# Two threshold digits per attention tile, and an expert layer written out

## The chip, the cores and the metric

The kernel runs on one core of a Trainium2 chip. The metric is the device time of one execution in microseconds. Before the change it was 1450.71 us, the median of three runs (1446.56 to 1451.18).

## The reference, cut to what matters

Input x has shape (4, 1024, 256). Four layers follow one another, each added to x: a cross attention, an expert layer with the two best experts of each token, a second cross attention with 16 heads over 77 keys, and an expert layer in which each expert chooses its tokens. The change touches the last two.

```python
def _L1_ffn_ref(x, gate_w, w_gate, w_up, w_down):
    k = S // E * CAPACITY                      # 256 tokens for each of 8 experts
    affinity = softmax(einsum('bsd,ed->bse', x, gate_w)).transpose(0, 2, 1)
    gating, idx = jax.lax.top_k(affinity, k)
    x_in = x[bidx, idx]
    h = silu(einsum('bekd,eid->beki', x_in, w_gate)) * einsum('bekd,eid->beki', x_in, w_up)
    x_e = einsum('beki,edi->bekd', h, w_down)
    return zeros_like(x).at[bidx, idx].add(gating[..., None] * x_e)
```

So before the first expert can start, the 256th largest affinity of every pair of batch and expert must be known.

## The kernel before, in words

**The search.** The four batches are handled as two halves (q = 0 and 1) of two batches each, so a search finds 16 thresholds (2 batches, 8 experts) at once. The threshold is built as the bits of a float, ten digits of three bits. For a digit, `count` on VectorE compares 1024 affinities a partition with a candidate and adds up (L1515, L1516); `choose_pe` on TensorE adds the passed candidates with a matmul of one column (L1439); `choose_dve` on VectorE turns the sum into the digit and the next candidate (L1523 to L1526). Each step waits for the one before it. After digit 9 come four more exchanges between the two engines: THR (threshold to all partitions, two masks, L1441, L1532), RANKS (prefix sums of the masks, L1445 to L1449, slot numbers and the one-hot arrays hotA and hotC, L1536 to L1544), FILL (matmul of the one-hots, L1455, own tokens, L1546 to L1549) and TURN (L1459, the index table gidx, L1554). GpSimd then gathers the rows of an expert with gidx (L2030).

**The attention.** `in_order` writes out 32 tiles of 128 rows with no loop. Each engine runs a list of named steps (PE_ORDER, DVE_ORDER and so on, L1580 to L1588), each with a lag: in iteration j the step works on tile j minus lag. TensorE runs about two iterations ahead of VectorE. The first search runs in it: its softmax at tile 19, `count` of digit 0 at tile 26, digits 0 to 4 with tiles 27 to 31 (FIRST_DIGIT, lag 2 on VectorE, with the scores on TensorE). Digits 5 to 9, THR and RANKS are in the table TAIL, after the last scores (`tail_a` and `tail_b`), while the last tiles are finished; I call this stretch the drain. FILL and TURN come in `topk_tensor` and `topk_vector`, after the last tile. There the second search (q = 1) also starts with its softmax and first count.

In an iteration VectorE computes, in this order: statistics and normalising, the residual of tile t (L1848, reads psO1), low halves of probabilities (L1817), maxima of the scores (L1825, L1834), the digit, the count. TensorE: transposes out, turn2, tail_a, outputs0, transposes in, scores0 (with the digit's matmul ahead), outputs1, turn0, outputs2, turn1, scores1, tail_b, logits. The logits (psL1) share a PSUM bank with psO1, and wait for the residual that reads it.

**The expert layer.** Sixteen items (expert and batch half), a step j does: `up` of item j-2 (8 blocks f0 to f7, 12 matmuls each), `transposes` of item j-1, `down` of item j-3 (4 blocks n0 to n3). ScalarE and VectorE split the weights in high and low f16 parts (L2112, L2172, L2122, L2181) and compute the hidden rows (L2136, L2196, L2209). `pipeline` writes steps 0 to 5 out, runs steps 6 to 13 in a loop of two turns of four steps, and writes out the rest. The second search is placed by the table LATER: (step, block) to exchange. Its exchange on TensorE comes right after that block; on VectorE after the block's hidden rows (f), ahead of the eight low parts of the down weights (n1) or behind them (n2, n3).

Of the kernel before, what the change touches and what calls it, by code (L numbers as in the profile page):

```python
# [31 lines left out]
P = 128  # L32
# [113 lines left out]
def program(nc, a, out, tab, n0_rows, x1_rows, n_rows):  # L146
    ctx = ExitStack()
    with ctx:
# [1266 lines left out]
        D_MASK = D_THR + 2  # L1415
        D_HOT = D_MASK + 7
        D_LIST = D_HOT + 3
# [92 lines left out]
        def count(dve, ch, q, i):  # L1510
# [5 lines left out]
            ch(dve.tensor_scalar(passed[:], cnt1[:], CAP - 0.5, None, ALU.is_ge))  # L1516

        def choose_dve(dve, ch, q, p, bank0, bank1):

# [14 lines left out]
            elif p == RANKS:  # L1534
# [4 lines left out]
                ch(dve.tensor_scalar(sc_[:], sloti[:], 15, None, ALU.bitwise_and))  # L1539
                nums = iota16[:].unsqueeze(1).to_broadcast([P, NI * RB, 16])  # L1540
                ch(dve.tensor_tensor(hotA[:], sa[:].unsqueeze(2).to_broadcast([P, NI * RB, 16]), nums, ALU.is_equal))
                ch(dve.tensor_tensor(hotC[:], sc_[:].unsqueeze(2).to_broadcast([P, NI * RB, 16]), nums, ALU.is_equal))
                values = hotC[:].rearrange("p (i c) n -> p i (c n)", i=NI)
                ch(dve.tensor_tensor(values, values, tokv[:].unsqueeze(2).to_broadcast([P, NI, RB * 16]), ALU.mult))  # L1544
            elif p == FILL:
# [5 lines left out]
            else:  # L1551
                for b in range(2):
# [11 lines left out]
        ROWS_AT = ((0, 23), (1, 24), (0, 24), (1, 25))  # L1564
        TAIL = {(27, "a"): 5, (27, "b"): 6, (28, "a"): 7, (28, "b"): 8, (29, "a"): 9, (29, "b"): THR, (30, "a"): RANKS}
        c_one = sem("c_one")
# [4 lines left out]
        PE_ORDER = [("transposes_out", 5), ("turn2", 3), ("tail_a", 6), ("outputs0", 3), ("transposes_in", 0), ("scores0", 1),  # L1571
                    ("outputs1", 3), ("turn0", 2), ("outputs2", 3), ("turn1", 2), ("scores1", 0), ("tail_b", 6), ("logits", 6)]
        ACT_ORDER = [("exps1", 2), ("probs_high0", 3), ("shares_exp", 5), ("exps0", 2), ("probs_high1", 3), ("copy_out", 5),
                     ("high_in", 0), ("weights_high", 0), ("shares_copy", 5), ("probs_high2", 3)]
        DVE_ORDER = [("stats_in", 0), ("normalise_out", 6), ("moments_in", 0), ("residual", 5), ("shares_max", 5), ("probs_low0", 4),
                     ("tail_a", 7), ("stats_out", 5), ("moments_out", 5), ("largest1", 2), ("reciprocals", 3), ("probs_low1", 4),
                     ("maxima1", 2), ("low_in", 1), ("probs_low2", 4), ("largest0", 2), ("digit", 2), ("maxima0", 2),
# [124 lines left out]
        def attn1_tensor(pe):  # L1702
# [14 lines left out]
            def scores(half):  # L1717
                def run(t, par):
                    pe.wait_ge(c_xl, t + 1)
                    wait(pe, c_exp[half], t)  # L1720
                    if (half, t) in ROWS_AT:
                        rows_pe(pe, 0, ROWS_AT.index((half, t)), inA[2 * half:2 * half + 2])
                    if half == 0 and t >= FIRST_DIGIT:
                        choose_pe(pe, 0, t - FIRST_DIGIT, inA[0], inA[1])
                    for q in (2 * half, 2 * half + 1):
                        for k in range(KD):
                            at = bass.ds((t // (S // P)) * (KD * CK) + (k * CK + q * QK), QK)
                            last = mm3(pe, psS1[:, q, 0:QK], xh1[:, par, k, :], xl1[:, par, k, :],
                                       M1hf[:, at], M1lf[:, at], k == 0, k == KD - 1)
                    last.then_inc(c_sc[half], 1)  # L1730
                return run

            def logits(t, par):
                pe.wait_ge(c_xe, t + 1)
                wait(pe, c_res, before(t, "logits", "outputs0", PE_ORDER, T))
                for k in range(KD):
                    last = pe.matmul(psL1[:, bass.ds(t * E, E)], xt1[:, par, k, :], gts1[:, k, :], start=(k == 0), stop=(k == KD - 1))
                last.then_inc(c_lg, 1)
# [24 lines left out]
            def tail(name):  # L1763
                def run(t, par):
                    if (t, name) not in TAIL:
                        return
                    for n in range(2):
                        pe.wait_ge(c_exp[n], T)
                    choose_pe(pe, 0, TAIL[t, name], drain0, drain1)
                return run  # L1770
            M1hf = M1h[:].rearrange("p b k c -> p (b k c)")
            M1lf = M1l[:].rearrange("p b k c -> p (b k c)")
            N1f = N1[:].rearrange("p b c d -> p (b c d)")
            steps = dict(tail_a=tail("a"), tail_b=tail("b"), transposes_in=transposes(0), transposes_out=transposes(1), scores0=scores(0), scores1=scores(1),
                         turn0=turn(0), turn1=turn(1), turn2=turn(2), logits=logits,
# [6 lines left out]
        def attn1_vector(dve):  # L1782
# [59 lines left out]
            def residual(t, par):  # L1842
                row = X[:, bass.ds(t, 1), :].rearrange("p t d -> p (t d)")
                dve.wait_ge(c_av[2], t + 1)
                if t == 19:
                    dve.wait_ge(c_lg, T // 2)
                    soft_max(dve, ch, 0)
                dve.scalar_tensor_tensor(row, psO1, thx1[:, 0:1], row, ALU.mult, ALU.add).then_inc(c_res, 1)  # L1848

# [11 lines left out]
            def digit(t, par):  # L1861
                if t >= FIRST_DIGIT:
                    choose_dve(dve, ch, 0, t - FIRST_DIGIT, inA[0], inA[1])

            def counts(t, par):
                if t >= FIRST_DIGIT - 1:
                    count(dve, ch, 0, t - FIRST_DIGIT + 1)

            def tail(name):
                def run(t, par):  # L1870
                    if (t, name) not in TAIL:
                        return
                    p = TAIL[t, name]
                    choose_dve(dve, ch, 0, p, drain0, drain1)
                    if p + 1 < DIGITS:
                        count(dve, ch, 0, p + 1)
                return run
# [22 lines left out]
            def weights_low(t, par):  # L1900
                f = t - 4
                if not 0 <= f < FT1:
# [6 lines left out]
            ch = Chain(dve, k_dve, 0, KSTEPS)  # L1909
            steps = dict(shares_max=shares_max, shares_div=shares_div, digit=digit, count=counts, tables=tables,  # L1910
                         tail_a=tail("a"), tail_b=tail("b"), weights_low=weights_low,
                         probs_low0=probs_low(0), probs_low1=probs_low(1), probs_low2=probs_low(2),
# [4 lines left out]
            in_order(dve, steps, DVE_ORDER, T, straight=True)  # L1917
            return ch

# [43 lines left out]
        second0, second1 = psXb[:, 0, :], psXb[:, 1, :]  # L1963
        LATER = {(2, "f2"): 0, (2, "f5"): 1, (3, "f2"): 2, (3, "f5"): 3, (3, "n1"): 4, (3, "n2"): 5, (3, "n3"): 6,
                 (4, "f2"): 7, (4, "f5"): 8, (4, "n1"): 9, (4, "n2"): THR, (4, "n3"): RANKS, (5, "f5"): FILL, (5, "n1"): TURN}

# [17 lines left out]
        def topk_tensor(pe):  # L1984
            choose_pe(pe, 0, FILL, drain0, drain1)
            choose_pe(pe, 0, TURN, drain0, drain1)
            for n in range(ROWS):
                rows_pe(pe, 1, n, [psYb[:, n, k * P:(k + 1) * P] for k in range(2)])

        def topk_vector(dve, first):  # L1990

            second = Chain(dve, k_dve, 1, KSTEPS)
            dve.wait_ge(c_lg, T)
            choose_dve(dve, first, 0, FILL, drain0, drain1)
            choose_dve(dve, first, 0, TURN, drain0, drain1)
            soft_max(dve, second, 1)
# [54 lines left out]
        def ffn1_tensor(pe):  # L2051
            def transposes(j, ph):
                par = ph % 2
                pe.wait_ge(d_in[par], 16 * NT * (j // 2) + 16 * NT)
                wait(pe, d_xl, KD * j)
                p = later(j + 1, "f5") if isinstance(j, int) else None
                if p is not None:
# [40 lines left out]
            for n in range(2):  # L2098
                pe.wait_ge(c_exp[n], T)
            pipeline(pe, NB1, DD, [(2, up), (1, transposes), (3, down)], unroll=4)  # L2100

        def ffn1_scalar(act):
# [58 lines left out]
            work += [(1, up_high(f, False)) for f in range(FT1)] + [(2, down_high(f)) for f in range(FT1)]  # L2161
            pipeline(act, NB1, DD, work + [(3, results)], unroll=4)

        def ffn1_vector(dve, ch):
# [47 lines left out]
            def choose(lag, name):  # L2212
                def run(j, ph):
# [4 lines left out]
                    if p + 1 < DIGITS:  # L2218
                        count(dve, ch, 1, p + 1)
                return run  # L2220
            work = [(2, hidden(0)), (1, up_low(0, True))]
            for f in range(1, FT1):
                work += [(2, hidden(f)), (2, hidden_low(f - 1)), (1, up_low(f, True)), (2, choose(2, f"f{f - 1}"))]
            work += [(2, hidden_low(FT1 - 1)), (1, rows_low)]
            work += [(1, up_low(f, False)) for f in range(FT1)]
            work += [(3, choose(3, "n1"))] + [(2, down_low(f)) for f in range(FT1)] + [(3, choose(3, "n2")), (3, choose(3, "n3"))]
            pipeline(dve, NB1, DD, work, unroll=4)

        with nc.Block() as block:
# [36 lines left out]
            def _(dve):  # L2266
                attn0_vector(dve)
                ffn0_vector(dve)
                prep_vector(dve)
                first = attn1_vector(dve)  # L2270
                second = topk_vector(dve, first)
                ffn1_vector(dve, second)
# [51 lines left out]
```

## Time and profile before

| | us |
|---|---|
| median of three runs | 1450.71 |
| the profiled execution's own time | 1452.21 |
| its span, first to last instruction | 1450.5 |
| TensorE busy in the span | 1317.3 (91%) |
| VectorE busy | 912.1 (63%) |
| ScalarE busy | 759.9 (52%) |
| GpSimd busy | 625.2 (43%) |

The profile is of one execution. The granted clock of TensorE is 1.00 at full speed and 0.50 at half. By the trace the second attention's tiles run up to about 834 us, the drain to 893.6, the expert layer from there to the end. A busy share says how much an engine works, not whether anyone waits for it; for that the waits and the order in time are read.

### The profile page before, as it was taken

How to read it: one execution, taken by the hardware profiler on the slowest of the kernel's cores; microseconds unless marked ns; L12 is line 12 of the kernel's file. 1: busy time of each engine (PE TensorE's matmuls, PEld its weight loads, DVE VectorE, ACT ScalarE, POOL GpSimd, SP SyncE). 2: the span in 40 equal slices, each digit the busy share in tenths (PEclk: the TensorE clock that was granted, in tenths of full speed). 3: DMA queues.
4: the chain of work that ended last, by engine and by line, in shares of the span. 5: the costliest groups of instructions: out<-in, count | busy, mean ns of one | idle time of the engine just before them, and what ended most of it. 6: DMA issues, size and time to landing. Idle time of an engine off the chain costs nothing.

```text
span 1450.5 us, 29512 instructions
## 1 busy us (share of the span) xinstructions
PE 1317.3 (91%) x9858; PEld 988.9 (68%) x9859; DVE 912.1 (63%) x2123; ACT 759.9 (52%) x2313; POOL 625.2 (43%) x664
## 2 busy tenths in 40 slices
PE   6877699999999987999999965898999989999997
PEld 3766588889999856888888853355656646665555
DVE  2887664565554585778777855777655646655551
ACT  3765322433323365988878812444555646655552
POOL 2187777656666531554444413123233332233313
PEclk8665699999999989999999976999999999999998
DMA  5658445653333341000200102233333333444422
GB/s 145 215 146 201 76 50 70 134 87 62 61 65 61 52 124 59 23 31 31 95 31 30 33 29 76 102 117 117 117 117 117 117 118 117 123 159 158 130 44 30
DMA packets 81547, 133.20 MB, mean 92 GB/s; under 512 B 24662, under 2 KB 71260, under 8 KB 76316
## 3 DMA queue, kind: packets, MB, share of 16 engines
q1 hardware_dynamic: 51132, 93.92, 19.8%
q0 software_dynamic: 29312, 37.57, 15.6%
q8 instruction: 64, 1.05, 0.3%
q14 instruction: 47, 0.39, 0.1%
q10 hardware_dynamic: 992, 0.27, 0.1%
HBM read 95.08 MB, written 36.65 MB: 91 GB/s over the span
## 4 chain that ended last, share of the span: by engine, by line
PE 71%; DVE 10%; DMA 7%; issue 4%; POOL 4%; ACT 3%; SPq 1%; POOLq 0%; ACTq 0%; DVEq 0%
PE psG L124 5%; PE psG L125 5%; PE psG L126 5%; PE psU L124 5%; PE psU L126 5%; PE psU L125 5%; PE psYb L126 3%; PE psYb L124 3%; PE psYb L125 3%; DMA stage<-in_w 2%; PE psS L124 2%; PE psS L125 2%; PE psS L126 2%; PE psP L1747 2%; PE psOL L124 2%
## 5 line engine op out<-in xcount | busy, mean ns | idle before, releaser
L2045 POOL DMA_INDIRECT out_x<-yo,gidx x64 | 107.6, 1681 | 343.3 <-ACT yo L2147 327.3
L2196 DVE SCALAR_TENSOR_TENSOR hid<-psU,sil 128x512 f32<-128x512 f32 x128 | 88.4, 691 | 198.1 <-ACT sil L2136 197.8
L2136 ACT ACTIVATE sil<-psG 128x512 f32<-128x512 f32 x128 | 76.4, 597 | 217.5 <-PE psU L126 217.5
L980 POOL DMA_INDIRECT x_rows<-yo,tabs x78 | 124.4, 1594 | 94.9 <-ACT yo L1052 71.1
L1673 ACT ACTIVATE pr<-psS,mx 128x77 f32<-128x77 f32 x512 | 158.8, 359 | 0.8 <-DVE mx L1834 0.8
L125 PE MATMUL psYb<-W1dl,hh 128*128 128x256 f16 x512 | 140.4, 274 | 0.0
L124 PE MATMUL psYb<-W1dh,hh 128*128 128x256 f16 x512 | 140.4, 274 | 0.0
L126 PE MATMUL psYb<-W1dh,hl 128*128 128x256 f16 x512 | 140.3, 274 | 0.0
L1079 DVE SCALAR_TENSOR_TENSOR hid<-psU,sil 128x512 f32<-128x512 f32 x78 | 53.8, 690 | 127.7 <-ACT sil L1043 127.6
L1673 ACT ACTIVATION_READ_ACCUMULATOR pr<-psS,mx 128x1 f32 x512 | 123.7, 242 | 0.0
L1043 ACT ACTIVATE sil<-psG 128x512 f32<-128x512 f32 x78 | 46.5, 596 | 133.1 <-PE psU L126 133.1
L970 POOL DMA_INDIRECT bx<-n_rows,tabs x78 | 82.5, 1058 | 26.0 <-issue 21.9
L124 PE MATMUL psOL<-N,pt 128*128 128x256 f16 x320 | 89.2, 279 | 3.1 <-DVE pt L1817 3.1
L124 PE MATMUL psG<-bxh,Wh 128*128 128x256 f16 x312 | 85.6, 274 | 4.6 <-DVE bxl L1070 4.6
L2030 POOL DMA_INDIRECT gx<-n_rows,gidx x64 | 64.0, 1001 | 59.5 <-DVE gxl L2189 24.5
L125 PE MATMUL psOL<-N,pt 128*128 128x256 f16 x320 | 89.3, 279 | 0.0
L126 PE MATMUL psOL<-N,pt 128*128 128x256 f16 x320 | 89.2, 279 | 0.0
L2209 DVE TENSOR_TENSOR hl<-hid,hh 128x512 f16<-128x512 f32 x128 | 87.7, 685 | 1.7 <-ACT hh L2155 0.2
L124 PE MATMUL psU<-bxh,Wh 128*128 128x256 f16 x312 | 85.6, 274 | 0.0
L125 PE MATMUL psG<-bxl,Wh 128*128 128x256 f16 x312 | 85.6, 274 | 0.0
L126 PE MATMUL psU<-bxh,Wl 128*128 128x256 f16 x312 | 85.6, 274 | 0.0
L125 PE MATMUL psU<-bxl,Wh 128*128 128x256 f16 x312 | 85.6, 274 | 0.0
(403 smaller groups left out, 4189.5 us busy)
## 6 DMA issues: line engine op xcount, KB each, us to landing
w1u<-in_w SPq DMA_DIRECT2D x16, 2048.0 KB, 7.5
w1d<-in_w SPq DMA_DIRECT2D x16, 1024.0 KB, 8.1
stage<-in_w SPq DMA_DIRECT2D x8, 1536.0 KB, 8.7
X<-in_x SPq DMA_DIRECT2D x8, 512.0 KB, 8.9
n_rows<-xc SPq DMA_DIRECT2D x8, 512.0 KB, 9.5
x_rows<-X SPq DMA_DIRECT2D x8, 512.0 KB, 12.0
X<-x_rows SPq DMA_DIRECT2D x8, 512.0 KB, 8.1
out_x<-X SPq DMA_DIRECT2D x32, 128.0 KB, 1.7
```

What stands on the lines that cost most here:

```text
L124: pe.matmul(o, lh, rh, start=first, stop=False)
L125: pe.matmul(o, lh, rl, start=False, stop=False)
L126: return pe.matmul(o, ll, rh, start=False, stop=stop)
L970: pool.indirect_dma_start(bx[:, par, n, :], None, n0_rows[:, :], bass.IndirectOffsetOnAxis(tabs[:, j, n, 0:1], 0)).then_inc(b_in[par], 16)
L980: pool.indirect_dma_start(x1_rows[:, :], bass.IndirectOffsetOnAxis(tabs[:, j, n, 0:1], 0), yo[:, par, n, :], None, compute_op=ALU.add).the ...
L1079: dve.scalar_tensor_tensor(hid[:, half, :, :], psU[half][:, :, :], SH / (SX * SW), sil[:, half, :, :], ALU.mult, ALU.mult).then_inc(b_hid[ ...
L1673: ins = act.activation(pr1[:, par, h * LK:(h + 1) * LK], psS1[:, q, i * LK:(i + 1) * LK], ACT.Exp, bias=mx1[:, h:h + 1], scale=1.0 / (SX * ...
L2030: pool.indirect_dma_start(gx[:, j % 2, n, :], None, n_rows[0:2 * S * (j // E + 1), :], bass.IndirectOffsetOnAxis(gidx[:, half, col:col + 1 ...
L2045: pool.indirect_dma_start(out_rows[:, :], bass.IndirectOffsetOnAxis(gidx[:, half, col:col + 1], 0), yo1[:, j % 2, n, :], None, compute_op= ...
L2136: act.activation(sil1[:, f % 2, :], psG1[f % 2][:], ACT.Silu, scale=1.0 / (SX * SW)).then_inc(d_sil, 1)
L2196: dve.scalar_tensor_tensor(hid1[:, f % 2, :], psU1[f % 2][:], SH / (SX * SW), sil1[:, f % 2, :], ALU.mult, ALU.mult).then_inc(d_hid, 1)
L2209: dve.tensor_tensor(hl1[:, par, f, :], hid1[:, f % 2, :], hh1[:, par, f, :], ALU.subtract).then_inc(d_hl, 1)
```

## The change: what it does

First, in the attention's last five tiles a search takes an even digit where it took its only one before, and an odd digit in a new step `digit_odd`: on TensorE after turn1 and ahead of scores1, on VectorE after the residual, followed by `count_odd` after the first low half. Digits 0, 2, 4, 6, 8 come at tiles 27 to 31, digits 1, 3, 5, 7, 9 with the iterations of the residuals of tiles 25 to 29. The odd sum is written to psL1's bank, so the residual waits for the digit's matmul and the logits wait until the digit is read. THR, RANKS, FILL and TURN move into the drain. The one-hot work of RANKS (three operations on 2048 elements) becomes six on 1024, `one_hot_half`.

Second, the expert layer is written out on TensorE, ScalarE and VectorE (straight=True).

Third, the second search moves from steps 2 to 5 to steps 3 to 7, three exchanges a step, and its six one-hot halves go one behind each of the blocks f0 to f5 of step 7.

```diff
-        D_HOT = D_MASK + 7
+        D_HOT = D_MASK + 10
+        def one_hot_half(dve, ch, n):
+            half = slice((n % 2) * (NI * RB // 2), (n % 2 + 1) * (NI * RB // 2))
+            nums = iota16[:].unsqueeze(1).to_broadcast([P, NI * RB // 2, 16])
+            if n < 2:
+                ch(dve.tensor_tensor(hotA[:, half], sa[:, half].unsqueeze(2).to_broadcast([P, NI * RB // 2, 16]), nums, ALU.is_equal))
+            elif n < 4:
+                ch(dve.tensor_tensor(hotC[:, half], sc_[:, half].unsqueeze(2).to_broadcast([P, NI * RB // 2, 16]), nums, ALU.is_equal))
+            else:
+                values = hotC[:, half].rearrange("p (i c) n -> p i (c n)", i=NI // 2)
+                tiles = slice((n % 2) * (NI // 2), (n % 2 + 1) * (NI // 2))
+                ch(dve.tensor_tensor(values, values, tokv[:, tiles].unsqueeze(2).to_broadcast([P, NI // 2, RB * 16]), ALU.mult))
...
-        TAIL = {(27, "a"): 5, (27, "b"): 6, (28, "a"): 7, (28, "b"): 8, (29, "a"): 9, (29, "b"): THR, (30, "a"): RANKS}
+        FIRST_ODD = 25
+        TAIL_PE = {(27, "a"): THR, (28, "a"): RANKS, (29, "b"): FILL, (30, "b"): TURN}
+        TAIL_DVE = {(27, "a"): THR, (28, "b"): RANKS, (29, "b"): FILL, (30, "b"): TURN}
+        def even_of(t):
+            return 2 * (t - FIRST_DIGIT) if 0 <= t - FIRST_DIGIT < DIGITS // 2 else None
+        def odd_of(t):
+            return 2 * (t - FIRST_ODD) + 1 if 0 <= t - FIRST_ODD < DIGITS // 2 else None
...
-                    ("outputs1", 3), ("turn0", 2), ("outputs2", 3), ("turn1", 2), ("scores1", 0), ("tail_b", 6), ("logits", 6)]
+                    ("outputs1", 3), ("turn0", 2), ("outputs2", 3), ("turn1", 2), ("digit_odd", 3), ("scores1", 0), ("tail_b", 6), ("logits", 6)]
...
-        DVE_ORDER = [("stats_in", 0), ("normalise_out", 6), ("moments_in", 0), ("residual", 5), ("shares_max", 5), ("probs_low0", 4),
-                     ("tail_a", 7), ("stats_out", 5), ("moments_out", 5), ("largest1", 2), ("reciprocals", 3), ("probs_low1", 4),
+        DVE_ORDER = [("stats_in", 0), ("normalise_out", 6), ("moments_in", 0), ("residual", 5), ("digit_odd", 5), ("shares_max", 5), ("probs_low0", 4),
+                     ("count_odd", 5), ("tail_a", 7), ("stats_out", 5), ("moments_out", 5), ("largest1", 2), ("reciprocals", 3), ("probs_low1", 4),
...
+                if odd_of(t + 3) is not None:
+                    pe.wait_ge(k_dve, read_at(0, odd_of(t + 3)))
...
+                if odd_of(t) is not None:
+                    dve.wait_ge(k_pe, ROWS + odd_of(t) + 1)
                 dve.scalar_tensor_tensor(row, psO1, thx1[:, 0:1], row, ALU.mult, ALU.add).then_inc(c_res, 1)
...
+                    if p == RANKS:
+                        for n in range(6):
+                            one_hot_half(dve, ch, n)
...
-        LATER = {(2, "f2"): 0, (2, "f5"): 1, (3, "f2"): 2, (3, "f5"): 3, (3, "n1"): 4, (3, "n2"): 5, (3, "n3"): 6,
-                 (4, "f2"): 7, (4, "f5"): 8, (4, "n1"): 9, (4, "n2"): THR, (4, "n3"): RANKS, (5, "f5"): FILL, (5, "n1"): TURN}
+        LATER = {(3, "f4"): 0, (3, "n1"): 1, (3, "n2"): 2, (4, "f4"): 3, (4, "n1"): 4, (4, "n2"): 5,
+                 (5, "f4"): 6, (5, "n1"): 7, (5, "n2"): 8, (6, "f4"): 9, (6, "n1"): THR, (6, "n2"): RANKS,
+                 (7, "n1"): FILL, (7, "n2"): TURN}
+        ONE_HOT_STEP = 7
...
         def topk_tensor(pe):
-            choose_pe(pe, 0, FILL, drain0, drain1)
-            choose_pe(pe, 0, TURN, drain0, drain1)
...
-            choose_dve(dve, first, 0, FILL, drain0, drain1)
-            choose_dve(dve, first, 0, TURN, drain0, drain1)
...
-            pipeline(pe, NB1, DD, [(2, up), (1, transposes), (3, down)], unroll=4)
+            pipeline(pe, NB1, DD, [(2, up), (1, transposes), (3, down)], unroll=4, straight=True)
...
+            def one_hot(f):
+                def run(j, ph):
+                    if j + 2 == ONE_HOT_STEP and f < 6:
+                        one_hot_half(dve, ch, f)
+                return run
...
-                work += [(2, hidden(f)), (2, hidden_low(f - 1)), (1, up_low(f, True)), (2, choose(2, f"f{f - 1}"))]
+                work += [(2, hidden(f)), (2, hidden_low(f - 1)), (1, up_low(f, True)), (2, choose(2, f"f{f - 1}")), (2, one_hot(f - 1))]
```

## Rows read from the trace of the kernel before

**Rows 1.** The page's part 4, the chain's shares by engine.

```profile
PE 71%; DVE 10%; DMA 7%; issue 4%; POOL 4%; ACT 3%; SPq 1%; POOLq 0%; ACTq 0%; DVEq 0%
```

**Rows 2.** Windows, one attention tile: length, busy by engine, clock, DMA share, GB/s.

```profile
817.54:825.98 8.44, 8.44 (x76) 7.21 (x74) 7.22 (x21) 6.91 (x38) 3.33 (x5) 1.00 0.09 31
```

**Rows 3.** Timeline of VectorE: start, length, operation, and idle time with its releaser.

```profile
824.17 0.42 DVE L1810 SCALAR_TENSOR_TENSOR xl<-psXar,xh 128x256 f16<-128x256 f32 x1 [0.66 <-ACT xh L1648]
...
825.26 0.81 DVE L1825 TENSOR_REDUCE psS<-psS 128x8 f32<-128x616 f32 x1 [0.34 <-PE psS L126]
...
833.41 0.81 DVE L1825 TENSOR_REDUCE psS<-psS 128x8 f32<-128x616 f32 x1 [1.45 <-PE psS L126]
834.13 0.15 DVE L1523 TENSOR_SCALAR dig<-psS 128x1 int32<-128x1 f32 x1
...
836.35 0.41 DVE L1804 TENSOR_SCALAR xn<-X,mv,rs 128x256 f32<-128x256 f32 x1
```

**Rows 4.** Timeline of TensorE in the drain and at the first expert matmul.

```profile
842.03 0.36 PE L124 MATMUL psOL<-N,pt 128*128 128x256 f16 x1 [2.20 <-DVE pt L1817]
...
877.85 1.89 PE L1455 MATMUL psS<-hotC,hotA 128*128 128x128 f16 x16 [6.73 <-DVE hotC L1544]
...
893.61 0.61 PE L124 MATMUL psG<-gxh,upAh 128*128 128x512 f16 x1 [2.08 <-DVE gxl L2189]
```

**Rows 5.** Timeline of the drain, GpSimd and VectorE.

```profile
842.20 1.91 POOL L1620 TENSOR_TENSOR pn<-pr,sum 128x1024 f32<-128x1024 f32 x1
...
869.54 0.42 DVE L1536 SCALAR_TENSOR_TENSOR slot<-psS,mask 128x256 f32<-128x256 f32 x1 [2.60 <-PE psS L1449]
...
870.85 2.29 DVE L1541 TENSOR_TENSOR hotA<-sa,iota 128x2048 f16<-128x2048 int32 x1
...
882.80 1.12 POOL L2030 DMA_INDIRECT gx<-n_rows,gidx  x1 [16.37 <-DVE gidx L1554]
```

**Rows 6.** Timeline of TensorE: the transposes in expert steps 3 to 6.

```profile
945.54 1.04 PE L2061 MATMUL psXb<-ident,gx 128*128 128x128 f32 x8
...
983.12 1.04 PE L2061 MATMUL psXb<-ident,gx 128*128 128x128 f32 x8
...
1026.33 1.06 PE L2061 MATMUL psXb<-ident,gx 128*128 128x128 f32 x8
...
1058.47 1.04 PE L2061 MATMUL psXb<-ident,gx 128*128 128x128 f32 x8
```

**Rows 7.** Timeline of TensorE: its waits in expert steps 3 to 5.

```profile
922.18 0.61 PE L124 MATMUL psG<-gxh,upBh 128*128 128x512 f16 x1 [4.53 <-DVE gxl L2189]
...
957.40 0.16 PE L1439 MATMUL psXb<-passed,same 128*128 128x1 bf16 x1 [2.94 <-DVE passed L1516]
...
993.48 0.20 PE L1441 MATMUL psXb<-ident,thrb 16*128 16x16 f32 x1 [1.43 <-DVE thrb L1528]
...
1007.08 0.61 PE L124 MATMUL psG<-gxh,upBh 128*128 128x512 f16 x1 [3.98 <-DVE hid L2196]
```

**Rows 8.** Timeline of SyncE's load issues (one a step), and TensorE at step 10.

```profile
1163.64 0.33 SPq L1583 DMA_DIRECT2D w1u<-in_w  x1
...
1171.20 0.61 PE L124 MATMUL psG<-gxh,upAh 128*128 128x512 f16 x1 [4.99 <-issue]
...
1203.53 0.33 SPq L1583 DMA_DIRECT2D w1u<-in_w  x1
...
1331.82 0.33 SPq L1583 DMA_DIRECT2D w1u<-in_w  x1
...
1363.90 0.33 SPq L1583 DMA_DIRECT2D w1u<-in_w  x1
```

**Rows 9.** Timeline of VectorE in expert steps 3 and 6.

```profile
949.12 1.28 DVE L2189 SCALAR_TENSOR_TENSOR gxl<-psXb,gxh 128x512 f16<-128x512 f32 x2
...
955.14 0.15 DVE L1523 TENSOR_SCALAR dig<-psXb 128x1 int32<-128x1 f32 x1
...
1061.30 1.28 DVE L2189 SCALAR_TENSOR_TENSOR gxl<-psXb,gxh 128x512 f16<-128x512 f32 x2
```

More of the change, by code:

```diff
@@ L1539, in choose_dve @@
                 ch(dve.tensor_scalar(sc_[:], sloti[:], 15, None, ALU.bitwise_and))
[L1540 to L1544, printed above, removed]
             elif p == FILL:
@@ L1723, in run @@
                     if half == 0 and t >= FIRST_DIGIT:
-                        choose_pe(pe, 0, t - FIRST_DIGIT, inA[0], inA[1])
+                        choose_pe(pe, 0, even_of(t), inA[0], inA[1])
                     for q in (2 * half, 2 * half + 1):
@@ L1764, in run @@
                 def run(t, par):
-                    if (t, name) not in TAIL:
+                    if (t, name) not in TAIL_PE:
                         return
@@ L1768, in run, with digit_odd @@
                         pe.wait_ge(c_exp[n], T)
-                    choose_pe(pe, 0, TAIL[t, name], drain0, drain1)
+                    choose_pe(pe, 0, TAIL_PE[t, name], drain0, drain1)
                 return run
+            def digit_odd(t, par):
+                if odd_of(t) is not None:
+                    choose_pe(pe, 0, odd_of(t), psL1, None)
             M1hf = M1h[:].rearrange("p b k c -> p (b k c)")
@@ L1773, in attn1_tensor @@
             N1f = N1[:].rearrange("p b c d -> p (b c d)")
-            steps = dict(tail_a=tail("a"), tail_b=tail("b"), transposes_in=transposes(0), transposes_out=transposes(1), scores0=scores(0), scores1=scores(1),
+            steps = dict(tail_a=tail("a"), tail_b=tail("b"), digit_odd=digit_odd, transposes_in=transposes(0), transposes_out=transposes(1), scores0=scores(0), scores1=scores(1),
                          turn0=turn(0), turn1=turn(1), turn2=turn(2), logits=logits,
@@ L1847, in residual @@
                     soft_max(dve, ch, 0)
+                if odd_of(t) is not None:
+                    dve.wait_ge(k_pe, ROWS + odd_of(t) + 1)
                 dve.scalar_tensor_tensor(row, psO1, thx1[:, 0:1], row, ALU.mult, ALU.add).then_inc(c_res, 1)
@@ L1861, in digit, with digit_odd, count_odd @@
             def digit(t, par):
-                if t >= FIRST_DIGIT:
-                    choose_dve(dve, ch, 0, t - FIRST_DIGIT, inA[0], inA[1])
+                if even_of(t) is not None:
+                    choose_dve(dve, ch, 0, even_of(t), inA[0], inA[1])
             def counts(t, par):
-                if t >= FIRST_DIGIT - 1:
-                    count(dve, ch, 0, t - FIRST_DIGIT + 1)
+                if t == FIRST_DIGIT - 1:
+                    count(dve, ch, 0, 0)
+                if even_of(t) is not None:
+                    count(dve, ch, 0, even_of(t) + 1)
+            def digit_odd(t, par):
+                if odd_of(t) is not None:
+                    choose_dve(dve, ch, 0, odd_of(t), psL1, None)
+            def count_odd(t, par):
+                if odd_of(t) is not None and odd_of(t) + 1 < DIGITS:
+                    count(dve, ch, 0, odd_of(t) + 1)
             def tail(name):
                 def run(t, par):
-                    if (t, name) not in TAIL:
+                    if (t, name) not in TAIL_DVE:
                         return
-                    p = TAIL[t, name]
+                    p = TAIL_DVE[t, name]
                     choose_dve(dve, ch, 0, p, drain0, drain1)
-                    if p + 1 < DIGITS:
-                        count(dve, ch, 0, p + 1)
+                    if p == RANKS:
+                        for n in range(6):
+                            one_hot_half(dve, ch, n)
                 return run
@@ L1910, in attn1_vector @@
             steps = dict(shares_max=shares_max, shares_div=shares_div, digit=digit, count=counts, tables=tables,
+                         digit_odd=digit_odd, count_odd=count_odd,
                          tail_a=tail("a"), tail_b=tail("b"), weights_low=weights_low,
@@ L1917, in attn1_vector @@
             in_order(dve, steps, DVE_ORDER, T, straight=True)
-            return ch
         l1.close()
@@ L1984, in topk_tensor, with topk_vector @@
         def topk_tensor(pe):
-            choose_pe(pe, 0, FILL, drain0, drain1)
-            choose_pe(pe, 0, TURN, drain0, drain1)
             for n in range(ROWS):
                 rows_pe(pe, 1, n, [psYb[:, n, k * P:(k + 1) * P] for k in range(2)])
-        def topk_vector(dve, first):
+        def topk_vector(dve):
             second = Chain(dve, k_dve, 1, KSTEPS)
             dve.wait_ge(c_lg, T)
-            choose_dve(dve, first, 0, FILL, drain0, drain1)
-            choose_dve(dve, first, 0, TURN, drain0, drain1)
             soft_max(dve, second, 1)
@@ L2055, in transposes @@
                 wait(pe, d_xl, KD * j)
-                p = later(j + 1, "f5") if isinstance(j, int) else None
+                p = later(j + 1, "f4") if isinstance(j, int) else None
                 if p is not None:
@@ L2161, in ffn1_scalar @@
             work += [(1, up_high(f, False)) for f in range(FT1)] + [(2, down_high(f)) for f in range(FT1)]
-            pipeline(act, NB1, DD, work + [(3, results)], unroll=4)
+            pipeline(act, NB1, DD, work + [(3, results)], unroll=4, straight=True)
         def ffn1_vector(dve, ch):
@@ L2226, in ffn1_vector @@
             work += [(3, choose(3, "n1"))] + [(2, down_low(f)) for f in range(FT1)] + [(3, choose(3, "n2")), (3, choose(3, "n3"))]
-            pipeline(dve, NB1, DD, work, unroll=4)
+            pipeline(dve, NB1, DD, work, unroll=4, straight=True)
         with nc.Block() as block:
@@ L2269, in _ @@
                 prep_vector(dve)
-                first = attn1_vector(dve)
-                second = topk_vector(dve, first)
+                attn1_vector(dve)
+                second = topk_vector(dve)
                 ffn1_vector(dve, second)
```

## The prediction

> **What bounds the kernel now.** I read the chain of waits, then windows tile by tile, then the timelines of the drain and of expert steps 2 to 10. The chain's split by engine [rows 1] says TensorE 71%, VectorE only 10%, so a change to VectorE's work pays only where VectorE's searches are what TensorE waits for. There are four kinds of places.
>
> In an attention tile TensorE has no idle time: 8.44 of 8.44 us, VectorE 7.22, in the tile from 817.54 [rows 2]. VectorE's true waits there are 0.66 and 0.34 us, and 1.45 us in the last tile, where it waits for the scores [rows 3]. In the drain after the last tile (834.1 to 893.6) the order turns round: TensorE waits for digits and residuals that stand behind counts, then 6.73 us for the one-hot arrays, and the experts' first matmul starts at 893.61 [rows 4]. In the expert layer a step costs 32.08 us once it runs freely (1331.82 to 1363.90, written-out code) [rows 8]; the step from 945.54 to 983.12 takes 37.58 and the next 43.21 [rows 6], and step 10 takes 39.89 (1163.64 to 1203.53), with 4.99 us in which TensorE waits for nothing that the profile shows [rows 8].
>
> **Part 1: two digits a tile.** One digit is read, applied and counted in 2.15 us of VectorE (834.13 to 836.35, less 0.08 for the maxima between) [rows 3]. Before, digits 0 to 3 are read a tile apart each, digit 4 at 834.13 in the last tile, and digits 5 to 9 come after it. After, digits 0, 2, 4, 6, 8 are read at those points and 1, 3, 5, 7 between them: four more of 2.15, 8.6 us. VectorE's waits in the four tiles are 1.00, 1.00, 1.00 and 1.45 [rows 3], 4.45 in all, and they cover that much. So digit 8 is read at 834.13 + 8.6 - 4.45 = 838.25: the tiles grow by 4.1 us, from about 8.6 to 9.7.
>
> The new waits. TensorE takes the odd digit after its transposes and before the next scores, and must wait for VectorE's count; behind it stand the scores (1.57), logits, transposes and outputs of 1.3, some 4.5 us up to the next even digit. VectorE needs 4.2 us from that count to the next (normalising, residual, odd digit, one low half, count), then 2.8 us more before it wants the scores, which are there at 6.1. So each side keeps about 0.9 us of slack, and the period is VectorE's sum. The residual's new wait on TensorE costs nothing: 1.1 us of normalising lies between. TensorE idles 1.0 to 1.4 us a tile. Bounds: +2 (TensorE's gaps in the records give cover too) to +8.6 (no cover).
>
> **Part 2: the drain.** Clock at 0 when digit 8 is read. Count of digit 9 to 2.2; residual, digit 9 and its broadcast to 3.6; one low half to 4.2; threshold transposed and two masks to 5.4; statistics to 6.0. GpSimd's root and the normalising (1.91 and 0.69, first of them in [rows 5]) to 9.6. Transposes and outputs (1.9) to 11.5, residual, logits, transposes to 13.3, ranks 1.7 to 15.0. Before, each step of this kind had a digit round of 2.15 in it. VectorE then takes slots (869.54 to 870.85, 1.3) and six halves. A whole one-hot pass is 2.29 for 2048 elements and a 256-element one 0.42 [rows 5]; 1024 by the line between them is 1.22, and with 0.03 between instructions the six take 7.5: to 24.0. The halves stand ahead of the last residual, so outputs of tile 31 are hidden under them, and the logits, the transpose of tile 30 and the fill come after: residual 24.8, logits and transpose 26.2, fill 28.2 (1.89 at half clock [rows 4]), own tokens 30.1, normalise, transpose and turn 31.3, indices 32.0, gather 32.3. Before, the gather starts at 882.80 [rows 5], 48.7 after its digit 4. So 16.4 less, and 12.3 less net of the tiles: gather at 870.5.
>
> From gather to first expert matmul it was 10.8 us (882.80 to 893.61). The second search's softmax now starts 0.5 us later against it (it waits for the last logits), and has 1.9 us of slack. The down-weight load, before at 871.20, far ahead of the gather, now goes out beside it. It took 4.9 us alone, so at most the gather's first half meets it: I take 0.3, bounds 0 and 2. First matmul near 881.6; gain 12.0, bounds 7 and 16.
>
> The row gives half of 2.29, 1.15, if nothing is paid per instruction. Against this change speaks the Trainium skill (VectorE: DVE Perf Modes, "The TRN2 errata — SBUF-src ops pay a fixed extra latency per instruction"): about 151 cycles at 0.96 GHz come with every instruction, so many small tiles pay many times. By that, an estimate, a half is 1.224 us and six cost 7.3 before gaps against 6.9 by halving: 0.5 us lost by the split. It changes the total by less than its uncertainty.
>
> **Part 3: expert layer written out.** The loop covers steps 6 to 13 in two turns of four, so TensorE jumps back once, at step 10: 4.99 us of nothing, then half clock (first matmul 0.61 instead of 0.38) [rows 8]. Against the free step this is 39.89 - 32.08 = 7.8 us. No VectorE, ScalarE or load is late there. Written out it goes. The free 32.08 is of a step without a loop, so straight code has no price of its own that shows; ends 0 and 7.8, I take 7.8.
>
> **Part 4: second search in steps 3 to 7.** Step 2 loses its two digits (4.3 us of VectorE beside early weight conversions). TensorE waited 4.53 before 922.18 [rows 7]; without the digits VectorE's last hidden row starts 1.35 earlier and the 0.19 stall at 911 goes: 1.5 saved, the rest of the wait is the transposes' own path.
>
> Steps 3, 4, 5 each have a digit at f4, n1, n2. That at f4 is hidden: VectorE waits 1.3 a block there and recovers in two. The pair n1, n2 isn't: VectorE reads n1 only after eight low conversions (955.14), so n2 at TensorE waited 2.94 (957.40) [rows 7]. Now no digit at f5 delays this. Free, the low rows start 2.83 after the transposes (1061.30 against 1058.47), with f5 3.58 (949.12 against 945.54) [rows 6, 9]: 0.75 earlier, so the wait is 2.2. Does the clock fall? After 2.20 idle at 842.03 matmuls went from 0.27 to 0.36, then 0.42 [rows 4]; after 1.43 at 993.48 it held [rows 7]. I say it falls, 1.75 more each as in the 3.5 us at half clock after 957.4. Three steps: 3 x 3.95 = 11.9. Step 6: threshold 0.7 (masks instead of a count), ranks 1.3; step 7: fill 1.1, wait 0.6, turn 0.2; its halves of 1.25 fit under the 1.3 of wait a block. Sum 15.8, against (37.58 - 32.08) + (43.21 - 32.08) = 16.6 now, in which the one-hots alone held TensorE 3.98 (1007.08) [rows 7]. Saved 0.8; bounds +6 (clock holds) and -4 (every one falls, halves not quite hidden).
>
> **Sum.** 12.0 + 7.8 + 1.5 + 0.8 = 22.1. The profiled execution took 1452.21 (span 1450.5), 1.5 over the median of 1450.71; applied to the median: 1428.6, I say 1429.
>
> **Rivals.**
> (a) The clock falls in the tiles. TensorE now idles over 1 us in each of four or five tiles; if that is enough to halve its clock, its 8.4 us of work become some 15, and a tile 15.3 instead of 9.7. Four and a half tiles cost 25 and outweigh 22: 1454. It decides at the point where an idle time of 1.0 to 1.4 a tile lowers the granted clock from 1.00. Against: 1.43 at 993.48 didn't. For: such gaps would repeat every tile. 6%.
> (b) The clock holds after 2.2 us waits in steps 3 to 5, and in the drain too: 5.2 and 3 more, 1420 to 1423. 13%.
> (c) The halves, the fill behind the last residual and the load beside the gather eat half of the drain's gain (no VectorE cover in the tiles 4.4, gather 2): 1435 to 1440. 13%.
> (d) The 7.8 isn't the jump. Step 10 is also the first with an expert of the second batch half; then it stays, and 1437. Against: its rows were ready (VectorE had done everything of the step by 1166.3). 7%.
> (e) The change doesn't shorten the drain at all because something older binds (the second search's start, the weight load): gain of 10 only, 1441 or more, up to no change. 6%.
>
> **Chances.** Main case (1424 to 1434) 55%, rivals as above. What can be told from no change is 0.3%, 4.4 us. Below 1446: 0.90; within: 0.04; above 1455: 0.06, mostly (a). Range 1419 to 1441: it takes in (b), (c), (d).
>
> **What would show it.** Digit 8 read near 838.3; TensorE clock 1.00 through the tiles; gather near 870.5 and first expert matmul near 881.6; six 1.2 us passes between 854 and 862, TensorE idle under them; step 10 at 32.1; steps 3 to 5 at about 36, 6 and 7 at 34. Wrong if the tiles take over 10 us each, if TensorE's clock is at half in them, or if step 10 keeps a 5 us gap.

## The result, and the profile after

The changed kernel takes 1424.47 us (median of four, 1421.16 to 1426.59) against 1450.91 before (four runs, 1446.56 to 1451.18). The ratio is 0.9821, 95% interval 0.9803 to 0.9839: 26.4 us faster. Forecast was 1429.

The profiled execution took 1426.59 us with a span of 1424.8. By stage it stands against before like this (each number is a difference of two starts; the first count of the search is the common start, 791.73 before and 794.06 after):

| stretch | before | after | change | forecast |
|---|---|---|---|---|
| start to first count | 791.73 | 794.06 | +2.3 | 0 |
| first count to the last tile's digit | 42.40 | 46.38 | +4.0 | +4.1 |
| that digit to the first gather | 48.67 | 30.98 | -17.7 | -16.4 |
| gather to first expert matmul | 10.81 | 11.30 | +0.5 | +0.3 |
| first expert matmul to step 3's load | 61.64 | 58.07 | -3.6 | -1.5 |
| intervals 4 to 8 | 176.32 | 172.92 | -3.4 | -0.8 |
| interval 10 | 39.89 | 32.07 | -7.8 | -7.8 |

An interval is the time from one up-weight load to the next and has the number of the load that ends it; the loads go out late in a step, so interval 4 holds the down blocks of step 3. A load waits until VectorE has made the low parts of the weights before, so it goes out later where VectorE is late, though TensorE isn't. That is so at step 3's load of before (the parts end at 955.21, it goes out at 955.25): VectorE begins these parts 4.78 us after the transposes before (945.54 [rows 6]) and 4.02 after the change, and 0.8 of the 3.6 us is this. By the transposes, from which the prediction adds, the two lines are -2.8 and -4.2. Before:

```profile
950.32 4.89 DVE L2172 SCALAR_TENSOR_TENSOR upAl<-w1u,upAh 128x512 f16<-128x512 f32 x8
...
1122.62 1.04 PE L2061 MATMUL psXb<-ident,gx 128*128 128x128 f32 x8
```

After:

```profile
931.85 1.04 PE L2096 MATMUL psXb<-ident,gx 128*128 128x128 f32 x8
...
935.87 4.89 DVE L2207 SCALAR_TENSOR_TENSOR upAl<-w1u,upAh 128x512 f16<-128x512 f32 x8
...
1104.77 1.04 PE L2096 MATMUL psXb<-ident,gx 128*128 128x128 f32 x8
```

The first line of the table isn't the change's: the kernels do the same there, and its place moves between profiles of both attentions (789.74 to 794.24 over nine profiles).

The windows of three of the tiles with two digits, from the read of one even digit to the next (columns as in [rows 2]):

```profile
811.99:821.96 9.97, 9.04 (x76) 7.08 (x74) 9.59 (x30) 7.12 (x39) 4.12 (x8) 1.00 0.19 36
821.96:831.52 9.56, 8.90 (x76) 7.12 (x74) 9.18 (x27) 7.02 (x39) 3.32 (x6) 1.00 0.08 27
831.52:840.44 8.92, 8.31 (x71) 6.71 (x70) 8.54 (x26) 6.32 (x36) 3.01 (x6) 1.00 0.10 32
```

The roles of [rows 2] have changed: VectorE (third) is busy 9.59 of 9.97 us with no wait shown, TensorE (first) has 0.9 us idle, and its clock stays at 1.00, the upper of its two levels (2.4 GHz).

The drain on VectorE. To be seen: the last even digit (840.44, answering to 834.13 in [rows 3]), the residual of tile 30 after a wait for its outputs, slots and six halves in a row (two in each line), the residual of tile 31 behind them, the indices.

```profile
840.44 0.15 DVE L1536 TENSOR_SCALAR dig<-psS 128x1 int32<-128x1 f32 x1
...
852.18 0.48 DVE L1874 SCALAR_TENSOR_TENSOR X<-psOL,thx,X 128x256 f32<-128x256 f32 x1 [1.95 <-PE psOL L126]
...
854.88 0.42 DVE L1549 SCALAR_TENSOR_TENSOR slot<-psS,mask 128x256 f32<-128x256 f32 x1
...
856.19 2.48 DVE L1523 TENSOR_TENSOR hotA<-sa,iota 128x1024 f16<-128x1024 int32 x2
858.71 2.48 DVE L1525 TENSOR_TENSOR hotC<-sc_,iota 128x1024 f16<-128x1024 int32 x2
861.22 2.48 DVE L1529 TENSOR_TENSOR hotC<-hotC,tokv 128x1024 f16<-128x1024 f16 x2
863.75 0.41 DVE L1828 TENSOR_SCALAR xn<-X,mv,rs 128x256 f32<-128x256 f32 x1
864.08 0.48 DVE L1874 SCALAR_TENSOR_TENSOR X<-psOL,thx,X 128x256 f32<-128x256 f32 x1
...
870.73 0.41 DVE L1562 TENSOR_SCALAR gidx<-psS 128x16 int32<-128x16 f32 x2 [0.82 <-PE psS L1459]
```

And on TensorE over the same stretch, with waits up to the first expert matmul (not all of them are shown), which answers to 893.61 in [rows 4]:

```profile
853.72 0.27 PE L1445 MATMUL psS<-mask,tri 128*128 128x256 bf16 x1
...
864.70 0.99 PE L1757 MATMUL psOL<-gts,xt 128*128 128x8 f32 x4 [6.58 <-DVE X L1874]
866.00 1.91 PE L1455 MATMUL psS<-hotC,hotA 128*128 128x128 f16 x16
...
878.70 1.94 PE L2096 MATMUL psXb<-ident,gx 128*128 128x128 f32 x8 [0.81 <-DMA gx<-n_rows,gidx]
882.72 0.61 PE L124 MATMUL psG<-gxh,upAh 128*128 128x512 f16 x1 [2.08 <-DVE gxl L2224]
```

TensorE still waits 6.58 us for the one-hot work; the profile gives the residual as the cause, since it stands behind the halves on VectorE. The halves take 856.19 to 863.75, 7.56 us, where three whole passes took 6.95 (870.85 [rows 5] to 877.80): the split costs 0.6. By the Trainium skill (VectorE: DVE Perf Modes, "The TRN2 errata — SBUF-src ops pay a fixed extra latency per instruction") three more instructions were estimated to cost 0.5, and the trace agrees: a fixed cost is there, and 0.6 in all.

The gather starts at 871.42 (882.80 before [rows 5]), where the timeline of GpSimd shows

```profile
871.42 1.12 POOL L2065 DMA_INDIRECT gx<-n_rows,gidx  x1 [5.23 <-DVE gidx L1562]
```

and 7.28 us later TensorE has its rows (878.70), against 6.78 before: the weight load at 872.48 beside it costs at most 0.5.

In the experts, TensorE's waits in steps 3 to 5, which answer to [rows 7]:

```profile
909.41 0.61 PE L124 MATMUL psG<-gxh,upBh 128*128 128x512 f16 x1 [3.54 <-DVE gxl L2224]
...
942.94 0.16 PE L1439 MATMUL psXb<-passed,same 128*128 128x1 bf16 x1 [2.17 <-DVE passed L1516]
...
979.09 0.16 PE L1439 MATMUL psXb<-passed,same 128*128 128x1 bf16 x1 [2.18 <-DVE passed L1516]
...
1013.57 0.16 PE L1439 MATMUL psXb<-passed,same 128*128 128x1 bf16 x1 [2.17 <-DVE passed L1516]
```

Each wait for the count is there, 2.2 us as worked out. What differs is the clock behind them. Windows of TensorE behind the three waits for the count (length, busy, clock, DMA share, GB/s):

```profile
943.00:946.00 3.00, 3.00 (x19) 0.59 0.99 421
...
979.00:982.00 3.00, 2.91 (x27) 1.00 1.01 426
...
1013.50:1016.00 2.50, 2.43 (x24) 1.00 0.99 419
```

After the first wait of 2.17 the clock fell, to 0.59 on average; after those of 2.18 and 2.17 it stayed. So interval 4 takes 36.15 us, intervals 5 and 6 34.5.

### The profile page after: what moved, and what is told of

Same layout as the page of the kernel before. It is cut to its first block, busy times and chain, and to the rows that moved or that the text cites. A ratio compares the mean times of both kernels' runs of the same rounds, so it can differ in the third digit from the quotient of the medians.

```text
span 1424.8 us, 29209 instructions
## 1 busy us (share of the span) xinstructions
PE 1300.5 (91%) x9858; PEld 977.7 (69%) x9859; DVE 914.8 (64%) x2129; ACT 760.5 (53%) x2313; POOL 623.0 (44%) x664
## 3 DMA queue, kind: packets, MB, share of 16 engines
q0 software_dynamic: 29312, 37.57, 15.8%
## 4 chain that ended last, share of the span: by engine, by line
PE 72%; DVE 11%; DMA 5%; POOL 4%; issue 4%; ACT 3%; SPq 0%; POOLq 0%; ACTq 0%; DVEq 0%
PE psG L124 6%; PE psG L126 6%; PE psG L125 6%; PE psU L124 6%; PE psU L125 6%; PE psU L126 6%; PE psYb L124 3%; PE psYb L126 3%; PE psYb L125 3%; PE psS L124 2%; PE psP L1767 2%; DMA stage<-in_w 2%; PE psS L125 2%; PE psS L126 2%; PE psOL L126 2%
## 5 line engine op out<-in xcount | busy, mean ns | idle before, releaser
L124 PE MATMUL psOL<-N,pt 128*128 128x256 f16 x320 | 87.3, 273 | 0.7 <-DVE pt L1841 0.7
L125 PE MATMUL psOL<-N,pt 128*128 128x256 f16 x320 | 87.3, 273 | 0.0
L126 PE MATMUL psOL<-N,pt 128*128 128x256 f16 x320 | 87.2, 273 | 0.0
L126 PE MATMUL psG<-bxh,Wl 128*128 128x256 f16 x312 | 85.7, 275 | 0.0
```

What stands on the lines that cost most here:

```text
L124: pe.matmul(o, lh, rh, start=first, stop=False)
L125: pe.matmul(o, lh, rl, start=False, stop=False)
L126: return pe.matmul(o, ll, rh, start=False, stop=stop)
```

## The experiments

Seven kernels. Steps are timed by the same load intervals, in these texts too where a step's time is given; "first matmul" is the expert layer's first. The time of the kernel before was taken again beside each group of runs: 1450.43 us for e1 to e4, 1448.57 for e5 to e7.

**e1_pe_straight** and **e2_pe_loop2** change the kernel before in one line, TensorE's expert loop:

```diff
-            pipeline(pe, NB1, DD, [(2, up), (1, transposes), (3, down)], unroll=4)
+            pipeline(pe, NB1, DD, [(2, up), (1, transposes), (3, down)], unroll=4, straight=True)   # e1
+            pipeline(pe, NB1, DD, [(2, up), (1, transposes), (3, down)], unroll=2)                  # e2
```

> The kernel before with the expert layer written out on TensorE alone; ScalarE and VectorE keep their loops. Theory (TensorE's own jump back costs the 4.99 us and the half clock after it): step 10 falls from 39.89 to 32.1 us, the whole 7.8 us faster, ratio about 0.9946. Rival 1 (the jump of ScalarE or VectorE holds step 10, or all three do): step 10 stays above 35 us, under 4 us faster. Rival 2 (step 10 is slow as the first with an expert of the second batch half): it stays at 39.9, no change.

Measured: 1443.41 us, ratio 0.9941 (0.9907 to 0.9975). Interval 10 takes 32.07, and the others from 4 on are within 0.2 of before. SyncE's load issues at step 10:

```profile
1163.47 0.33 SPq L1583 DMA_DIRECT2D w1u<-in_w  x1
...
1195.54 0.33 SPq L1583 DMA_DIRECT2D w1u<-in_w  x1
```

So TensorE's loop alone held step 10 ([rows 8]: 39.89). The loops that ScalarE and VectorE kept show no cost there, and the expert of the second batch half isn't it either.

> The kernel before with TensorE's expert loop two steps long instead of four: five turns over steps 6 to 15, four jumps back (at steps 8, 10, 12, 14) instead of one. Theory (each jump back costs TensorE the same): gaps of about 5 us with half clock behind them at steps 8, 10, 12 and 14, 3 x 7.8 = 23 us slower, 1474, ratio 1.016. Rival (the price is that the loop's body of four steps has to be loaded again, and a body half as long needs it less or not): the gaps are clearly under 5 us or absent, and the kernel is between 8 us faster and 5 us slower.

Measured: 1441.91 us, ratio 0.9942 (0.9926 to 0.9957), so my theory falls and the rival holds: with four jumps back in place of one there is no gap at all. Steps 4 to 8 are those of before, and all from 9 to 15 take 32.07 or 32.08.

```profile
1165.84 0.33 SPq L1583 DMA_DIRECT2D w1u<-in_w  x1
...
1197.91 0.33 SPq L1583 DMA_DIRECT2D w1u<-in_w  x1
```

It isn't the jump that costs 5 us, but the jump back over a long body. Part 3 of the profile's page says as much. The instruction packets of queue q8 before, with the short loop, and written out (e1):

```profile
q8 instruction: 64, 1.05, 0.3%
```

```profile
q8 instruction: 48, 0.79, 0.2%
```

```profile
q8 instruction: 61, 1.00, 0.3%
```

Written-out code holds eight steps more than the short loop and reads 13 packets more, some 1.6 a step. The long loop holds four steps fewer than written-out code, which at 1.6 a step would be about 54 packets, but it read 64: its body was loaded again, the short one wasn't. Reading code alone shows no cost, since e1 reads 61 packets and has no gap; the gap comes where TensorE jumps back to code that has to be loaded again. By windows a step has 202 matmuls and about as many weight loads, so four steps are over 1600 instructions and two over 800 (waits and register instructions not counted).

The Trainium skill (Runtime: NRT & Kernel Launch, "Instruction fetch mechanics") has a taken branch stall where its target isn't in the current window of two pages. That only the longer jump stalls agrees with it. Its size of a page, 256 instructions, doesn't: the short body's 800 are more than two such pages, and it didn't stall. The measurement decides; where between the two lengths the limit lies no run here shows.

**e3_attention_only** is the changed attention with the expert layer of before (loops, LATER of before, one-hots in six halves at one place).

> The changed attention with its drain, and the expert layer of before (loops, second search in steps 2 to 5; the one-hot work there in six halves in one place instead of three whole operations). Theory by the trace after: the first expert matmul comes 13.2 us earlier than before, less 0.4 for the halves in step 4: 12.8 us faster, 1438, ratio 0.991. Rival (the time before the changed stage is longer in the changed kernel as such, 2.3 us in the two profiles): 10.5 us faster, and the first count of the search again 2 us later than in the kernel before.

Measured: 1437.97 us, ratio 0.9911 (0.9882 to 0.9940): 12.5 us faster. First count at 790.85, first matmul at 879.56, 88.71 later; before it was 101.88, in the changed kernel 88.66. The 13.2 us belong to the attention part, and the 2.3 us ahead of it to the execution. Its loop over four steps is kept, and interval 10 takes 39.52 us with 64 packets on q8, as before.

**e4_old_later** is the changed kernel with only the second search put back (the diff is cut; its six one-hot halves stand in one place behind RANKS):

```diff
-        LATER = {(3, "f4"): 0, (3, "n1"): 1, (3, "n2"): 2, (4, "f4"): 3, ...
+        LATER = {(2, "f2"): 0, (2, "f5"): 1, (3, "f2"): 2, (3, "f5"): 3, ...   # as before
```

> The changed kernel with the second search back at steps 2 to 5 (its one-hot work in six halves in one place), all else as changed, expert layer written out. Theory by the two traces: the placement is worth 3.6 us in steps 2 and 3 and 3.5 us in steps 4 to 8, so this is 7 us slower than the changed kernel: 1431.5, ratio to before 0.9866. Rival (my prediction's 1.5 + 0.8): 2.3 us slower than the changed kernel, 1427.

Measured: 1428.97 us, ratio 0.9855 (0.9822 to 0.9888), 4.5 by the medians; by the traces 6.7 (first matmul to the end 548.8 against 542.1). The interval is too wide to part 7 from 2.3 by the times; the traces do it. The stretch from the first matmul to the first load and intervals 3 to 8 are 28.0, 33.85, 37.6, 42.1, 32.0, 32.1, 32.1 against 24.9, 33.2, 36.2, 34.5, 34.5, 33.9, 33.9. But 1.4 of the 3.2 us in the first number isn't the placement's: TensorE's clock was at 0.50 for 5.7 us from the first matmul in e4 and for 2.8 in the changed kernel, ahead of the first exchange of the search in either. Without it 5.3 us are left for the placement, near the 4.9 of the two ratios (0.0034 of 1451).

**e5_third_at_f1** takes away what makes TensorE wait at n2:

```diff
-        LATER = {(3, "f4"): 0, (3, "n1"): 1, (3, "n2"): 2, (4, "f4"): 3, (4, "n1"): 4, (4, "n2"): 5,
-                 (5, "f4"): 6, (5, "n1"): 7, (5, "n2"): 8, (6, "f4"): 9, (6, "n1"): THR, (6, "n2"): RANKS,
+        LATER = {(3, "f1"): 0, (3, "f4"): 1, (3, "n1"): 2, (4, "f1"): 3, (4, "f4"): 4, (4, "n1"): 5,
+                 (5, "f1"): 6, (5, "f4"): 7, (5, "n1"): 8, (6, "f1"): 9, (6, "f4"): THR, (6, "n1"): RANKS,
                  (7, "n1"): FILL, (7, "n2"): TURN}
```

> The changed kernel with the second search's third exchange of a step moved from n2 to f1: f1, f4, n1 in steps 3 to 6, fill and turn stay at n1 and n2 of step 7. Theory (TensorE waits at n2 only because n1 is read after eight low conversions, and at f1 a digit hides under 1.3 us of wait a block): the three waits of 2.17 us go, with the 1.7 to 1.8 us of half clock behind one of them, and step 6 loses its wait too: steps 3 to 5 at 32.1 to 32.4 us, step 6 at 33.2, 9 us faster than the changed kernel: 1415.5, ratio to before 0.9758. Rival (VectorE has no room at f1, since it comes late out of the down weights): TensorE waits 1 to 2 us for hidden rows in up, and the gain is under 4 us.

Measured: 1413.17 us, ratio 0.9749 (0.9732 to 0.9766) where the changed kernel has 0.9821: some 10.4 us faster. The waits of TensorE from 885 to 1200, all that are left (total, times, longest):

```profile
PE psG L124 <- DVE gxl L2224: 3.5, 1, 3.5
PE psXb L1459 <- DVE turned L1557: 0.8, 1, 0.8
```

The steps from the third on are 31.56, 32.15, 32.15, 32.39, 33.09, 33.87. From first matmul to the end it is 532.6 against 542.1: 9.5 by the traces, 9 expected, and 9.3 of it lies in intervals 4 to 8 (163.65 against 172.92). VectorE has room at f1.

**e6_residual_first** puts the last residual behind two of the six halves:

```diff
...
                     if p == RANKS:
-                        for n in range(6):
-                            one_hot_half(dve, ch, n)
+                        one_hot_half(dve, ch, 0)
+                        one_hot_half(dve, ch, 1)
...
+            def halves_after(t, par):          # in DVE_ORDER right after ("residual", 5), lag 6
+                if t == 30:
+                    for n in range(2, 6):
+                        one_hot_half(dve, ch, n)
```

> The changed kernel with only the first two one-hot halves ahead of the last residual, the other four behind it. Theory (the residual of tile 31 and what TensorE has behind it, logits 1.0 and transposes 0.3, stand needlessly behind the halves): they run under the last four halves; VectorE's sum stays, the fill starts 1.3 us earlier, first expert matmul 1.3 us earlier, 1423, ratio 0.9813. Rival (VectorE waits for the outputs of tile 31 after two halves): the gain is lost in a wait, 0 to 1 us slower.

Measured: 1422.15 us, ratio 0.9808 (0.9793 to 0.9824). First count to first matmul is 87.10 against 88.66 us: 1.6 earlier, where the theory has 1.3. Against the changed kernel's 0.9821 the intervals overlap, so the time alone wouldn't show it.

**e7_both** has both edits.

> Both edits of the two runs before. Theory: they touch different stages and add up: 1.3 + 9 = 10.3 us faster than the changed kernel, 1414, ratio 0.975. Rival: under 5 us faster, if one of them fails.

Measured: 1412.97 us, ratio 0.9750 (0.9737 to 0.9764), the expected 0.975, though no faster than e5 alone. The drain's gain is there. To be seen: the residual between the halves without a wait.

```profile
855.26 2.48 DVE L1523 TENSOR_TENSOR hotA<-sa,iota 128x1024 f16<-128x1024 int32 x2
857.78 0.41 DVE L1828 TENSOR_SCALAR xn<-X,mv,rs 128x256 f32<-128x256 f32 x1
858.11 0.48 DVE L1874 SCALAR_TENSOR_TENSOR X<-psOL,thx,X 128x256 f32<-128x256 f32 x1
858.50 2.47 DVE L1525 TENSOR_TENSOR hotC<-sc_,iota 128x1024 f16<-128x1024 int32 x2
```

First count to first matmul is 87.23 us, against 88.65 in e5, 1.4 less. Half of that was given back by the load that ends interval 3 (58.52 us from the first matmul against 57.84): after the same wait of 3.5 us the granted clock fell in e7 and not in e5, while e5's first matmuls had the half clock for longer. That is one execution each; whether it is more than chance stays open. e5 and e7 beat both kernels, by 35.4 and 35.6 us against 1448.57 before.

## Why the prediction was right, and where its sizes were off

- **Tiles.** +4.0 against +4.1. That VectorE's own sum sets a tile of two digits, with 4.45 us of old waits as cover, held; no new wait shows on it until the residual at 843.46 waits 0.23.
- **Rival (a), the clock in the tiles.** It stayed at 1.00 with TensorE idle 0.6 to 0.9 us a tile.
- **Drain.** -17.7 against -16.4. The chain is the one told, and e3 gives the attention part by itself. Up to the ranks it is on time (13.3 after the digit). The terms mis-sized are the ranks, priced as at half clock (1.7) and done in 1.1 at full clock (853.72 to 854.84), and the stretch from the end of the last residual to the gather, 6.9 us instead of 7.5.
- **Gather to experts.** +0.5 against +0.3.
- **Loop.** -7.8 as forecast, and e1 shows it is TensorE's loop, so rival (d) falls. The reason I gave, a jump back as such, was wrong: e2 has four and pays for none. The number came out right because only the presence of this loop was changed.
- **Up to step 3.** By the transposes -2.8 (51.93 to 49.13 from the first matmul) against -1.5. The wait fell from 4.53 to 3.54 and two stalls of 0.2 went, 1.4 together, near the forecast. Another 1.0 is the clock: after 922.18 it was at half for 5.2 us, after 909.41 for 3.4 (3.0 and 2.8 at the first matmuls). This isn't the change's: e4, after the same wait of 4.54, had half clock for only 3.1. I can't assign the last 0.4.
- **Steps 3 to 7.** By the transposes -4.2 against -0.8. The step of the prediction that failed is "I say it falls", 1.75 us of half clock after each of three waits. The waits were 2.17, 2.18, 2.17 against 2.2; the clock fell after one. What the search adds to five free steps of 32.07 was 12.6 (931.85 to 1104.77) instead of 15.8, nearly all of it these two times 1.75; steps 6 and 7 at 33.9 were as worked out. What it added before was 16.7 (945.54 to 1122.62), against 16.6. Rival (b), whose clock holds after all three, was half true.
- **The other rivals.** (c) and (e), which take half or more of the drain's gain, fall with e3. In (a) no run shows the 15 us put for a tile's work at half clock.

By stage the changed kernel came out 5.9 us under the forecast. In the profiled execution the later start, 2.3 us, hid part of that, which is luck; by the medians the miss is 4.5. Most of the 5.9 is TensorE's clock: 3.5 in steps 3 to 5, 1.0 ahead of them, 0.6 at the ranks. That it all goes one way is this execution's: in e4 and e5 the half clock from the first matmul on lasted 5.7 us instead of 2.8, 1.4 us the other way.

## What to carry to other kernels

A serial search between two engines can be spread over the tiles of a stage ahead of it as long as the weaker engine's waits there cover it; add up that engine's waits in a tile before choosing how many digits go in. Where an exchange sits matters more than how many there are: behind eight conversions each cost TensorE 2.2 us, ahead of them (e5) none. A loop back over a long body should be looked up in the trace once, since the same loop with half the body cost nothing.

## What the runs showed of the hardware that I hadn't expected

- A jump back costs TensorE 5.0 us (and half clock after) when the body is four steps of over 400 instructions each, and nothing when it is two. In e3 the gap is there again.
- The granted clock isn't a function of the wait alone. After 2.17 us idle it fell in step 3, after 2.18 and 2.17 us in steps 4 and 5, with the same work ahead, it stayed. e6, with the same steps, does the same: it fell after the wait before 941.11 (0.70 over the next 3 us) and stayed at 1.00 after those before 977.27 and 1011.75. So it need not be chance, and what decides it stays open. After 3.5 us it fell in the changed kernel, e6 and e7, and stayed in e5. Estimates of 1.75 us for such waits have to be carried as a range from 0.
